# Two of four softmax attentions get a ring of four sequences instead of three, and their row maxima are scored 11 slots sooner

## The chip, the cores and the metric

The kernel runs on one core of one Trainium2 chip. The metric is the device time of one execution in microseconds. The engines are TensorE (PE, matmuls), VectorE (DVE), ScalarE (ACT), GpSimd (POOL) and SyncE (SP, which here only issues DMAs).

## The reference, cut to what matters

Four transformer layers on `x`, 16 sequences of 256 tokens by 128 features. Each layer is `x + gate * attention(norm(x))`, then `x + gate * ffn(norm(x))`; layer 2's second half is itself a small transformer layer with a second attention. The change touches the attention of layer 0 (called a0) and that inner attention of layer 2 (a4). Both are causal, with 16 heads of 8 features:

```
q, k, v = h @ wq, h @ wk, h @ wv            # a4: 4 key/value heads, rotary embedding on q and k
s    = where(causal, q @ k.T / sqrt(8), -inf)   # 256 x 256, for 16 sequences x 16 heads
attn = softmax(s)                               # a4; a0 has per-head gates folded into q
out  = (attn @ v) @ wo
```

## The kernel before

`attention_phase` runs one attention over all 16 sequences as a software pipeline. Every engine executes the same hand-written order: a function `step(t, m)` for one step `t`, which is a loop over slots `h` = 0 to 15. In slot `h` of step `t` each engine does what is planned there for sequences at different stages: `has(stage, t)` says whether sequence `t + stage` exists. Waits are `after(engine, signal, b, k)`, and each engine executes its list strictly in order. Steps -3 to 0 and 13 to 16 are written out; steps 1 to 12 are a hardware loop of four passes over three steps (`steps`). The places in SBUF form a ring of three (`m`, `t % 3`): `QH`, `KH` (queries and keys with their mask rows), `VX` (values), `H`, `CX`.

For one sequence, in order of stages:

- **Norm**, step b-3, slots 4 to 12: PE mean (L669), DVE `XC`, ACT `SQ`, PE variance (L674), DVE `VE`, POOL `RS`, DVE `DG`, PE broadcast (L680), DVE `XN` (L841), ACT `H` (L523).
- **Projection and split**, step b-2, from slot 0: PE q and k (L656/L657; with rotary embedding L653/L654 twice), DVE (L810 on; rotary L804/L805 and POOL L469), then in slot 4 ACT splits q and k into three bf16 parts in the single buffer `SPL` (L536, POOL L475, ACT L539, POOL L478). SP copies these into `QH`/`KH` with 6 DMAs (L436/L437) and, when those have landed, duplicates them inside with 6 more (L442/L444); the first issue of a sequence is L435. The signal for "all landed" is `parts_sent`. The ACT split of the next sequence waits for it, since `SPL` is single.
- **Maxima**, step b-1: PE computes scores (L587 to L589) of one head into one of three banks and DVE reduces them to row maxima `NM3` (L784, `maxima`). 16 heads lie in slots 0 to 12 (`score_slots=13`), so slots 4, 8 and 12 hold two and slots 13 to 15 none. In slots 8 (heads 0-7) and 13 (heads 8-15) DVE makes `NMQ`; two slots later PE turns them (L728), and three slots later ACT and DVE split them into `M2` (L559, L881) and POOL, after a tiny operation `GO` (L485), sends them into two rows of `QH` (L487). The signals are `m_sent[0]` and `m_sent[1]`.
- **Softmax**, step b: PE computes the transposed scores with the maxima already subtracted through those rows (`scores_t`, L605 to L607), ACT takes the exponential (L549), PE multiplies by the values (L628, `values`) every fourth slot, and output parts are turned (L635), divided (DVE L764/L770), projected (L707, L712) and added (DVE L873/L876) in the following slots and step b+1.

In slot 0 of step t, PE does, in this order:

```
after(pe, m_sent[0], t)        # scores_t(t, head 0): maxima of heads 0-7 landed in QH
after(pe, parts_sent, t + 1)   # scores(t + 1, head 0): parts of the next sequence landed
after(pe, h_ready, t + 2)      # projection of the one after
```

The `fill` copies on DVE (L740) write the constant mask rows of each ring place once.

Of the kernel before, what the change touches and what calls it, by code (L numbers as in the profile page):

```python
# [11 lines left out]
P = 128  # L12
F32 = mybir.dt.float32
BF16 = mybir.dt.bfloat16
ALU = mybir.AluOpType
# [244 lines left out]
def attention_phase(c, cfg):  # L260
# [24 lines left out]
    SCALE = float(HD) ** -0.5  # L285
    l = cfg["layer"]
    SRC, DST = cfg["src"], cfg["dst"]

    with ExitStack() as ctx:
        sb = lambda name, shape, dt=F32: c.sb(cfg["name"] + name, shape, dt, ctx)  # L290
        QH = sb("QH", [KROWS, 3, NH, T], BF16)
        KH = sb("KH", [KROWS, 3, HK, T], BF16)
        VX = sb("VX", [P, 3, 2 * SV // PK, 2 * PK, 16])
        PR = sb("PR", [P, 8, NC])
        XC, SQ, XN = (sb(n, [P, T]) for n in ("XC", "SQ", "XN"))
        H = sb("H", [P, 3, T])
# [12 lines left out]
        CX = sb("CX", [P, 3, 2, cfg["CW"] // VW, VW])  # L309
# [102 lines left out]
        @block.sync  # L412
        def _(sp):
            for dst, src in ((QC, "qrows"), (KC, "krows")):
                sp.dma_start(dst[32:P, :].bitcast(F32), c.ins[src if causal or dst is KC else "norows"]).then_inc(rows_in, 16)
            for dst, src in loads:
                sp.dma_start(dst, c.ins[src]).then_inc(w_in, 16)

            def step(t, m):
                if isinstance(t, int) and -2 <= t <= 0:  # L420
                    sp.wait_ge(zeroed, 2)
                    sp.wait_ge(rows_ready, 4 * (t + 2) + 2)
                if has(2, t):
                    b, j = t + 2, (m + 2) % 3
                    for r in range(R):
                        after(sp, st_ready, b - 3)
                        heads = slice(16 * r, 16 * r + 16)
                        kheads = slice(16 * r, 16 * r + min(HK, 16))
                        group = lambda n: slice(HD * n, HD * n + HD)
                        first_q, first_k = (0, 2, 4), (0, 1, 3)  # L430
                        for a, ready, sent in ((0, hi_ready, high_sent[r]), (1, mid_ready, mid_sent[r]), (2, lo_ready, parts_sent[r])):
                            after(sp, ready, b, r + 1)
                            if r == a == 0:
                                for z in range(2):
                                    sp.dma_start(QH[MAX0 + z:MAX0 + z + 1, j, :, :], ZR[:, :]).then_inc(parts_sent[0].sem, 16)  # L435
                            sp.dma_start(QH[group(first_q[a]), j, heads, :], SPL[:, r, a, 0, :]).then_inc(sent.sem, 16)  # L436
                            sp.dma_start(KH[group(first_k[a]), j, kheads, :], SPL[0:KR, r, a, 1, :]).then_inc(sent.sem, 16)  # L437
                        for a, sent in ((0, high_sent[r]), (1, mid_sent[r])):
                            after(sp, sent, b)
                            for n, pair in enumerate(PAIRS):  # L440
                                if pair[0] == a and n != first_q[a]:
                                    sp.dma_start(QH[group(n), j, heads, :], QH[group(first_q[a]), j, heads, :]).then_inc(parts_sent[r].sem, 16)  # L442
                                if pair[1] == a and n != first_k[a]:
                                    sp.dma_start(KH[group(n), j, kheads, :], KH[group(first_k[a]), j, kheads, :]).then_inc(parts_sent[r].sem, 16)  # L444
            steps(sp, step)

        @block.gpsimd
        def _(pool):
# [7 lines left out]
            def step(t, m):  # L456
                for h in range(NH):
                    if has(3, t):
                        b = t + 3
# [4 lines left out]
                    if has(2, t):  # L464
                        b = t + 2
# [14 lines left out]
                    for g in range(2):  # L480
                        back = L_HALF[g] // NH
                        if h == L_HALF[g] % NH and has(1 - back, t):
                            after(pool, mlo_ready, t + 1 - back, g + 1)
                            after(pool, go, t + 1 - back, g)
                            nc.gpsimd.tensor_tensor(GO[:, :], c.HALF[0:1, 0:2], c.HALF[0:1, 0:2], ALU.add).then_inc(go.sem, 1)  # L485
                            for a in range(2):
                                pool.dma_start(QH[MAX0 + a:MAX0 + a + 1, (m + 1 - back) % 3, g * HG:(g + 1) * HG, :], M2[:, g, a, :])\  # L487
                                    .then_inc(m_sent[g].sem, 16)
# [7 lines left out]
        def _(act):  # L496
# [12 lines left out]
            def step(t, m):  # L509
                for h in range(NH):  # L510
                    if has(3, t):
                        b = t + 3
# [6 lines left out]
                        if h == L_H:  # L519
                            after(act, xn_ready, b)  # L520
                            after(act, v_ready, b - 3)
                            scale, shift = (c.MOD[:, l, 1, one(b)], c.MOD[:, l, 0, one(b)]) if centered else (COL[:, 3:4], 0.0)
                            nc.scalar.activation(H[:, m, :], XN[:, :], ACT.Identity, bias=shift, scale=scale).then_inc(h_ready.sem, 1)  # L523
                    if has(2, t):
                        b = t + 2
                        if h == L_V + 1 and not cfg.get("bv"):
                            after(act, v_ready, b)
                            if isinstance(t, int) and t == -2:
                                act.wait_ge(vx_ones, 1)
                            after(act, pv_done, b - 3)  # L530
                            nc.scalar.copy(v_place((m + 2) % 3), v_source).then_inc(v_copied.sem, 1)
# [8 lines left out]
                    if has(-1, t):  # L540
                        b = t - 1
                        if diff and h == L_COMBINE:
                            after(act, dif_ready, b)
                            nc.scalar.activation(CSQ[:, :, :, :], CX[:, (m - 1) % 3, :, :, :], ACT.Square).then_inc(csq_ready.sem, 1)
# [25 lines left out]
        def _(pe):  # L570
# [6 lines left out]
            def scores(b, j, h):  # L577
# [3 lines left out]
                if h == 0 and isinstance(b, int) and b < 2:  # L581
                    pe.wait_ge(rows_ready, 4 + 8 * b)
# [55 lines left out]
            def step(t, m):  # L638
                for h in range(NH):
                    if has(0, t):  # L640
                        scores_t(t, m, h)
                    if has(1, t):
                        for n in heads_at(h):
                            scores(t + 1, (m + 1) % 3, n)
                    if has(2, t):
                        b, j = t + 2, (m + 2) % 3
# [18 lines left out]
                    if has(3, t):  # L665
                        b = t + 3
# [15 lines left out]
                    if burst_at(h) and has(burst_at(h)[1], t):  # L682
                        u, back = burst_at(h)
                        values(t + back, (m + back) % 3, u)
                    for s, back in late(h, turn_at):
                        if has(-back, t):
# [4 lines left out]
                            for g in range(2):  # L691
                                if turns_before(L_NMQ[g] + 2) == s and has(1 - back, t):
                                    after(pe, mlo_ready, t + 1 - back, g + 1)
                            turn(b, s)
                    if has(-1, t):
                        b = t - 1
                        if h == L_CTT:
# [6 lines left out]
                            for n in range(2):  # L704
                                for r in range(R2):
                                    src = CX[:, (m - 1) % 3, n, :, :].rearrange("p h d -> p (h d)")[:, r * P:(r + 1) * P]
# [7 lines left out]
                    for g in range(2 if has(1, t) else 0):  # L714
                        b = t + 1
                        if h == L_NMQ[g] + 2:
# [4 lines left out]
                            if has(0, t):  # L721
                                after(pe, cx_ready, t, turns_before(L_NMQ[g] + 2))
# [10 lines left out]
        def _(v):  # L733
# [56 lines left out]
            def step(t, m):  # L790
                for h in range(NH):
                    if has(2, t):
                        b = t + 2
                        for n in range(QK):
                            if h == L_QK[n] + 1:
                                if isinstance(t, int) and t == -2 and n == 0:
# [19 lines left out]
                        if h == L_V + 1 and cfg.get("bv"):  # L816
                            after(v, v_ready, b)
                            if isinstance(t, int) and t == -2:
                                v.wait_ge(vx_ones, 1)
                            after(v, pv_done, b - 3)  # L820
                            bv = BV[:, :].rearrange("p (h d) -> p h d", h=SV).unsqueeze(1).to_broadcast([P, 2, SV, VW])
                            v.tensor_tensor(v_place((m + 2) % 3), v_source, bv, ALU.add).then_inc(v_copied.sem, 1)
                    if has(3, t):
                        b = t + 3
# [18 lines left out]
                    if has(1, t):  # L843
                        b = t + 1
                        for n in heads_at(h):
                            maxima(b, n)
                        for g in range(2):
                            heads = slice(g * HG, (g + 1) * HG)
                            if h == L_NMQ[g] and causal:
# [4 lines left out]
                    if has(-1, t):  # L854
# [7 lines left out]
                        if diff and h == L_CTT - 1:  # L862
                            after(v, cr_ready, b)
                            cx = CX[:, (m - 1) % 3, :, :, :]
# [17 lines left out]
                    for s, back in late(h, turned_at):  # L882
                        if has(-back, t):
                            turned(t - back, (m - back) % 3, s)
# [1058 lines left out]
def build(nc, ins, out):  # L1943

    with ExitStack() as ctx:
# [8 lines left out]
        attention_phase(c, dict(ln, name="a0", score_slots=13, layer=0, NH=16, HK=16, HV=16, VW=8, CW=128, causal=True,  # L1954
# [13 lines left out]
        attention_phase(c, dict(name="a4", score_slots=13, layer=2, centered=False, eps=rms["neps"], NH=16, HK=16, HV=4, VW=8, CW=128,  # L1968
# [115 lines left out]
```

## Time and profile before

| | us |
|---|---|
| median of 3 runs (lowest, highest) | 4036.28 (4019.64, 4040.5) |
| the profiled execution, its span | 4006.55, 4004.7 |
| a0: first head score to last value matmul | 65.1 to 389.8 |
| a4: first head score to last value matmul | 2481.6 to 2863.9 |

Busy time of an engine says how much work it has; what matters for a pipelined phase is how long one step takes and what PE waits for at its start. The granted clock of TensorE is 1.00 at 2.4 GHz and 0.50 at 1.2 GHz.

### The profile page before, as it was taken

Reading aid. Unit: us, or ns where it says so; the run is one execution under the profiler, and the core shown is the slowest. Engines: PE = TensorE matmul, PEld = TensorE weight load, DVE = VectorE, ACT = ScalarE, POOL = GpSimd, SP = SyncE. Lnnn points to the kernel's source line nnn. Section 1 sums busy time; section 2 is a strip of 40 time slices with the busy share of each in tenths; the row PEclk is TensorE's granted clock in tenths of the full one; section 3 lists DMA queues with packets and bytes.
Section 4 is the critical chain, followed back from the end, with each engine's and each line's share of the span. In section 5 each row is a group of like instructions: output and inputs, shape, how many; then the busy total and the mean of one; then the engine's idle time right before and its main releaser. Section 6 shows DMA issues by size and latency. Waiting matters only on the chain. (4 is left out here: it accounts for less than half of the span.)

```text
span 4004.7 us, 71964 instructions
## 1 busy us (share of the span) xinstructions
PE 3023.2 (75%) x20738; PEld 1870.4 (47%) x20738; DVE 2388.8 (60%) x5571; ACT 1445.8 (36%) x3108; POOL 915.0 (23%) x976
## 2 busy tenths in 40 slices
PE   5787433158888876999978986777779984459799
PEld 4555433146655653444435554555634461145344
DVE  5665841178887854333347765555555579984555
ACT  2555100026555534333326661444432221113321
POOL 2222118633333320000002222223200034430000
PEclk6899766569999988999989996888889985569899
DMA  3332313434333310000001111222100000000000
GB/s 70 41 42 42 109 38 55 63 63 53 44 48 45 41 49 3 1 0 0 0 8 27 23 19 21 34 33 35 39 2 0 0 3 0 0 5 22 4 0 21
DMA packets 125781, 111.13 MB, mean 28 GB/s; under 512 B 25177, under 2 KB 115938, under 8 KB 121570
## 3 DMA queue, kind: packets, MB, share of 16 engines
q1 hardware_dynamic: 103474, 93.91, 13.7%
q0 software_dynamic: 20912, 12.58, 2.1%
q8 instruction: 127, 2.08, 0.2%
q10 hardware_dynamic: 1152, 1.61, 0.1%
q14 instruction: 116, 0.95, 0.1%
HBM read 35.28 MB, written 13.86 MB: 12 GB/s over the span
## 5 line engine op out<-in xcount | busy, mean ns | idle before, releaser
L1408 DVE TENSOR_TENSOR f1eHS<-f1eSG,bank 128x512 f32<-128x512 f32 x256 | 175.9, 687 | 319.8 <-PE bank L1336 234.5
L1314 PE MATMUL bank<-f1NT,f1W 128*128 (+1 forms) x576 | 296.4, 596 | 15.8 <-DMA f1eSELB<-in_sel 15.3
L549 ACT ACTIVATE a1PR<-bank 128x384 f32<-128x384 f32 x512 | 242.8, 493 | 149.0 <-PE bank L607 145.1
L1336 PE MATMUL bank<-f1eHS,f1W 128*128 128x512 f32 x576 | 293.8, 592 | 0.0
L784 DVE TENSOR_REDUCE a1NM<-bank 128x3 f32<-128x384 f32 x512 | 262.8, 549 | 28.4 <-PE bank L589 25.7
L1367 ACT ACTIVATE f1eSG<-bank,f1eFB 128x512 f32<-128x512 f32 x256 | 175.8, 687 | 283.5 <-PE bank L1314 161.7
L784 DVE TENSOR_REDUCE a4NM<-bank 128x3 f32<-128x384 f32 x256 | 132.9, 551 | 136.8 <-PE bank L589 134.7
L787 DVE TENSOR_REDUCE a2NMQ<-bank 128x2 f32<-128x512 f32 x256 | 168.1, 685 | 60.6 <-PE bank L593 60.4
L953 PE MATMUL bank<-ONES 128*128 128x256 bf16 x960 | 172.0, 287 | 24.2 <-DMA f3nWR<-in_wr 4.6
L784 DVE TENSOR_REDUCE a0NM<-bank 128x3 f32<-128x384 f32 x256 | 133.8, 551 | 94.7 <-PE bank L589 93.5
L549 ACT ACTIVATE a4PR<-bank 128x384 f32<-128x384 f32 x256 | 122.3, 489 | 187.0 <-PE bank L607 186.4
L549 ACT ACTIVATE a2PR<-bank 128x512 f32<-128x512 f32 x256 | 149.6, 596 | 91.6 <-PE bank L611 89.5
L1314 PEld LDWEIGHTS bank<-f1NT,f1W 128*128 128x128 f32 x576 | 109.2, 191 | 156.2 <-issue 154.5
L1336 PEld LDWEIGHTS bank<-f1eHS,f1W 128*128 128x128 f32 x576 | 109.4, 190 | 130.1 <-issue 120.3
L549 ACT ACTIVATE a0PR<-bank 128x384 f32<-128x384 f32 x256 | 121.7, 490 | 133.5 <-PE bank L607 132.8
L1502 POOL TENSOR_TENSOR lM<-lF,lV 128x1024 f32<-128x1024 f32 x32 | 122.2, 3819 | 166.7 <-DVE lF L1515 166.2
L605 PE MATMUL bank<-a1QH,a1KH 128*128 128x128 bf16 x512 | 116.6, 229 | 57.0 <-ACT a1PR L549 42.6
L1367 ACT ACTIVATE f2eSG<-bank 128x512 f32<-128x512 f32 x96 | 57.3, 597 | 192.9 <-PE bank L1314 179.7
L1403 DVE TENSOR_TENSOR f3eT<-f3eSG,bank 128x512 f32<-128x512 f32 x88 | 60.5, 688 | 107.3 <-PE bank L1317 97.0
L1367 ACT ACTIVATE f3eSG<-bank 128x512 f32<-128x512 f32 x88 | 52.6, 597 | 190.0 <-PE bank L1314 190.0
L449 POOL MEMSET a2ZR<- 16x256 bf16 x1 | 0.3, 302 | 526.5 <-POOLq L1262 526.5
L953 PEld LDWEIGHTS bank<-ONES 128*128 128x128 bf16 x960 | 100.6, 119 | 42.5 <-issue 8.5
(633 smaller groups left out, 8613.5 us busy)
## 6 DMA issues: line engine op xcount, KB each, us to landing
a1QH<-a1SPL SPq DMA_DIRECT2D x96, 64.0 KB
a1KH<-a1SPL SPq DMA_DIRECT2D x96, 64.0 KB
a1QH<-a1QH SPq DMA_DIRECT2D x96, 64.0 KB
a1KH<-a1KH SPq DMA_DIRECT2D x96, 64.0 KB
f1W<-in_w SPq DMA_DIRECT2D x2, 2304.0 KB, 10.8
sums<-rZT SPq DMA_DIRECT2D x2, 2112.0 KB
sW<-in_w SPq DMA_DIRECT2D x1, 4096.0 KB, 12.5
xLD<-sums SPq DMA_DIRECT2D x16, 256.0 KB, 5.7
```

What stands on the lines that cost most here:

```text
L449: nc.gpsimd.memset(ZR[:, :], 0.0).then_inc(zeroed, 1)
L549: nc.scalar.activation(PR[:, h % 8, :], bank[2 + h % 2][:, 0:NC], ACT.Exp, scale=SCALE)\
L605: pe.matmul(o[:, 0:P], k(0), q(0), start=True, stop=True)
L784: v.tensor_reduce(NM3[:, h, :], S_BANK[h % 3][:, 0:NC].rearrange("p (n k) -> p n k", n=3), AX, ALU.max, negate=True).then_inc(s_used.sem, 1)
L787: v.tensor_reduce(NMQ[:, :, h], S_BANK[h % 3][:, 0:NC].rearrange("p (n k) -> p n k", n=2), AX, ALU.max, negate=True).then_inc(s_used.sem, 1)
L953: pe.matmul(bank[7][:, 0:2 * P], spare[:, 0:P], spare[:, :], start=True, stop=True)
L1314: pe.matmul(bank[q][:, :], W1[:, m * P:(m + 1) * P], x, start=True, stop=True).then_inc(g_ready.sem, 1)
L1336: mm = pe.matmul(bank[6 + j][:, :], W2[:, m, :], HS[:, m % 4, :], start=(m == 0), stop=(m == NCH - 1 and CBF is None))
L1367: nc.scalar.activation(dst, bank[q][:, :], fn, bias=FB[:, m:m + 1] if cfg.get("hbias") else 0.0)\
L1403: v.tensor_tensor(T1[:, :], a, bank[2 + q][:, :], ALU.mult).then_inc(t1_ready.sem, 1)
L1408: v.tensor_tensor(HS[:, m % 4, :], a, bank[4 + (j * NBC + kth[m]) % 2][:, :], ALU.mult).then_inc(hs_ready.sem, 1)
L1502: nc.gpsimd.tensor_tensor(M1[:, j, :, :, :], fk, vv, ALU.mult).then_inc(m1.sem, 1)
```

## The change

For a0 and a4 alone (`ring=4`, `score_slots=16`), the ring has four places, norm runs in step b-4, projection and split in step b-3, and the maxima's scores start 11 slots sooner: heads 0 to 10 of sequence t+2 in slots 5 to 15 of step t, and heads 11 to 15 of sequence t+1 in slots 0 to 4, one head in every slot. The maxima of heads 0-7 go out in slot 0 of step b-1 (they did in slot 11), those of heads 8-15 in slot 11 of step b-1 (they did in slot 0 of step b); the slots with `NMQ`, turn, `M2` and POOL DMAs stay 8/10/11 and 13/15/0, only which half of the heads uses them changes. Written out are steps -4 to 0 and 9 to 16; the loop has two passes over four steps. The other two attentions keep ring 3 and their order.

```diff
+    RING = cfg.get("ring", 3)
+    FRONT = RING - 1
-        QH = sb("QH", [KROWS, 3, NH, T], BF16)
+        QH = sb("QH", [KROWS, RING, NH, T], BF16)
...
+        LOOPS = (NB - 1 - RING) // RING
         def steps(eng, step):
-            for t in range(-3, 1):
-                step(t, t % 3)
-            with eng.Fori(0, 4) as i:
-                for k in range(1, 4):
-                    step(i * 3 + k, k % 3)
-            for t in range(13, 17):
-                step(t, t % 3)
+            for t in range(-RING, 1):
+                step(t, t % RING)
+            with eng.Fori(0, LOOPS) as i:
+                for k in range(1, RING + 1):
+                    step(i * RING + k, k % RING)
+            for t in range(LOOPS * RING + 1, 17):
+                step(t, t % RING)
...
-        L_SCORES = 0
+        L_SCORES = 0 if RING == 3 else -11
+        scores_at = lambda h: [(n, a) for a in (1, 2) for n in heads_at(h - NH * (a - 1))]
+        LAST_FILLED = 1 if RING == 3 else 2
-        L_NMQ = [16, 28] if diff else [8, 13]
+        L_NMQ = [16, 28] if diff else [8, 13] if RING == 3 else [-3, 8]
+        ahead = lambda slot: 1 - slot // NH
...
# SP, ACT, DVE, PE: projection, split and DMAs move from has(2, t) to has(FRONT, t), norm from has(3, t) to has(RING, t)
# PE, and in the same way maxima() on DVE:
-                    if has(1, t):
-                        for n in heads_at(h):
-                            scores(t + 1, (m + 1) % 3, n)
+                    for n, a in scores_at(h):
+                        if has(a, t):
+                            scores(t + a, (m + a) % RING, n)
...
# PE, turn of the maxima:
-                            if g:
-                                after(pe, mlo_ready, b, g)
+                            if g or RING > 3:
+                                after(pe, mlo_ready, b - (g == 0), 1 if g else 2)
...
-                            fill(t + 4, (part,))
+                            fill(t + RING + 1, (part,))
...
-        attention_phase(c, dict(ln, name="a0", score_slots=13, layer=0, ...
+        attention_phase(c, dict(ln, name="a0", score_slots=16, ring=4, layer=0, ...
-        attention_phase(c, dict(name="a4", score_slots=13, layer=2, ...
+        attention_phase(c, dict(name="a4", score_slots=16, ring=4, layer=2, ...
```

## Rows read from the trace of the kernel before

**Rows 1.** Busy time by stretch: a2 (the third attention), a0, a4.

```profile
core 0: us, PE busy (x) PEld busy (x) DVE busy (x) ACT busy (x) POOL busy (x), PEclk, DMA share, GB/s
...
2112.00:2402.00 290.00, 261.68 (x2438) 160.92 (x2436) 217.69 (x470) 192.17 (x388) 79.53 (x134) 0.98 0.14 23
85.00:390.00 305.00, 241.35 (x2930) 178.98 (x2929) 194.06 (x516) 168.65 (x401) 80.43 (x134) 0.92 0.28 39
2503.00:2864.00 361.00, 263.82 (x2963) 191.40 (x2963) 196.30 (x531) 162.64 (x401) 99.31 (x162) 0.86 0.24 33
```

**Rows 2.** PE's waits in a0, then in a4: us in total, times, longest.

```profile
PE bank L605 <- DMA a0QH<-a0M: 31.7, 14, 4.0
PE bank L680 <- DVE a0DG L837: 12.9, 12, 1.1
PE bank L635 <- DVE a0M L881: 10.0, 15, 0.7
...
PE bank L605 <- DMA a4QH<-a4M: 53.8, 15, 4.0
...
PE bank L587 <- DMA a4KH<-a4KH: 7.0, 7, 3.2
```

**Rows 3.** SP's first DMA issue of a sequence, by time: start, duration.

```profile
88.29 1.71 SPq L435 DMA_DIRECT2D a0QH<-a0ZR  x2
...
249.63 1.18 SPq L435 DMA_DIRECT2D a0QH<-a0ZR  x2
...
347.73 1.18 SPq L435 DMA_DIRECT2D a0QH<-a0ZR  x2
...
2512.64 1.18 SPq L435 DMA_DIRECT2D a4QH<-a4ZR  x2
...
2654.85 1.18 SPq L435 DMA_DIRECT2D a4QH<-a4ZR  x2
...
2821.86 1.19 SPq L435 DMA_DIRECT2D a4QH<-a4ZR  x2
```

**Rows 4.** Timeline at slot 0 of steps of a0 and a4: start, duration, idle before.

```profile
265.48 0.23 PE L605 MATMUL bank<-a0QH,a0KH 128*128 128x128 bf16 x1 [0.73 <-DMA a0QH<-a0M]
...
2664.22 1.09 POOL L487 DMA_DIRECT2D a4QH<-a4M  x2 [0.25 <-issue]
...
2669.81 0.29 PE L605 MATMUL bank<-a4QH,a4KH 128*128 128x128 bf16 x1 [3.52 <-DMA a4QH<-a4M]
...
2834.48 0.22 PE L605 MATMUL bank<-a4QH,a4KH 128*128 128x128 bf16 x1 [3.03 <-DMA a4QH<-a4M]
...
2837.49 0.26 PE L587 MATMUL bank<-a4KH,a4QH 128*128 128x128 bf16 x1 [2.68 <-DMA a4KH<-a4KH]
```

**Rows 5.** Landing of a4's maxima DMAs issued in 2663 to 2667, then 2671 to 2675.

```profile
DMA to landing us min/median/max: 2.2/3.6/5.0
...
DMA to landing us min/median/max: 1.6/1.6/1.6
```

**Rows 6.** Stretches (columns of rows 1): a0, its wait; a4 cold, warm, waiting.

```profile
226.10:243.20 17.10, 14.61 (x190) 11.07 (x190) 13.18 (x35) 10.87 (x26) 5.55 (x9) 1.00 0.37 48
243.20:245.00 1.80, 0.00 (x0) 0.00 (x0) 0.00 (x0) 0.00 (x0) 0.00 (x0) 0.87 0.01 2
2646.00:2651.00 5.00, 4.88 (x33) 3.04 (x34) 2.10 (x5) 1.22 (x3) 1.93 (x4) 0.51 0.01 2
2651.00:2666.30 15.30, 12.59 (x162) 9.58 (x160) 11.15 (x31) 9.28 (x23) 4.98 (x7) 1.00 0.35 43
2666.30:2669.80 3.50, 0.00 (x0) 0.00 (x0) 0.00 (x0) 0.03 (x1) 0.00 (x0) 0.74 0.17 42
```

**Rows 7.** SP's first issue of a sequence in a2, steps 1 to 6 of its loop.

```profile
2134.79 1.18 SPq L435 DMA_DIRECT2D a2QH<-a2ZR  x2
2153.27 1.18 SPq L435 DMA_DIRECT2D a2QH<-a2ZR  x2
2172.09 1.18 SPq L435 DMA_DIRECT2D a2QH<-a2ZR  x2
2190.60 1.19 SPq L435 DMA_DIRECT2D a2QH<-a2ZR  x2
2209.08 1.19 SPq L435 DMA_DIRECT2D a2QH<-a2ZR  x2
2227.58 1.19 SPq L435 DMA_DIRECT2D a2QH<-a2ZR  x2
```

**Rows 8.** The ramp of a0: first scores, second split, first softmax matmul.

```profile
65.06 0.29 PE L587 MATMUL bank<-a0KH,a0QH 128*128 128x128 bf16 x1 [7.86 <-DMA a0KH<-a0KH]
...
68.20 0.62 ACT L536 CAST a0SPL<-a0QKF 128x512 bf16<-128x512 f32 x1 [9.91 <-DVE a0QKF L815]
...
84.12 0.29 PE L605 MATMUL bank<-a0QH,a0KH 128*128 128x128 bf16 x1 [3.99 <-DMA a0KH<-a0KH]
```

**Rows 9.** DVE in a0: a maximum, a norm operation, a fill of the keys' rows.

```profile
L784 DVE TENSOR_REDUCE a0NM<-bank 128x3 f32<-128x384 f32 x164 | 86.2, 552 | 53.3 <-PE bank L589 52.5
...
L841 DVE TENSOR_TENSOR a0XN<-a0XC,bank 128x256 f32<-128x256 f32 x10 | 4.2, 421 | 0.0
...
L740 DVE COPY a0KH<-a0KC x6: 1216/1222/1354, 31.4 to 57.7; 32x4096 bf16<-32x4096 bf16 x3, 64x4096 bf16<-64x4096 bf16 x3
```

**Rows 10.** Steps 14 and 15 of a0, without projection, norm and copies.

```profile
363.50:378.80 15.30, 13.99 (x178) 9.85 (x178) 10.87 (x28) 8.92 (x22) 2.37 (x6) 0.89 0.01 3
378.80:391.50 12.70, 9.62 (x135) 5.68 (x132) 2.82 (x9) 8.23 (x21) 1.19 (x3) 0.99 0.02 3
```

More of the change, by code:

```diff
@@ L308, in attention_phase @@
         RC = sb("RC", [P, 2, 4 * PK])
[L309 removed]
+        CX = sb("CX", [P, RING, 2, cfg["CW"] // VW, VW])
         CTT = sb("CTT", [P, R2, T])
@@ L419, in step @@
             def step(t, m):
-                if isinstance(t, int) and -2 <= t <= 0:
+                if isinstance(t, int) and -FRONT <= t <= 0:
                     sp.wait_ge(zeroed, 2)
-                    sp.wait_ge(rows_ready, 4 * (t + 2) + 2)
-                if has(2, t):
-                    b, j = t + 2, (m + 2) % 3
+                    sp.wait_ge(rows_ready, 4 * (t + FRONT) + 2)
+                if has(FRONT, t):
+                    b, j = t + FRONT, (m + FRONT) % RING
                     for r in range(R):
-                        after(sp, st_ready, b - 3)
+                        after(sp, st_ready, b - RING)
                         heads = slice(16 * r, 16 * r + 16)
@@ L457, in step @@
                 for h in range(NH):
-                    if has(3, t):
-                        b = t + 3
+                    if has(RING, t):
+                        b = t + RING
                         if h == L_VE:
@@ L463, in step @@
                             nc.gpsimd.tensor_tensor(RS[:, :], VE[:, :], c.HALF[:, 0:2], ALU.pow).then_inc(rs_ready.sem, 1)
-                    if has(2, t):
-                        b = t + 2
+                    if has(FRONT, t):
+                        b = t + FRONT
                         for n in range(2 if rope else 0):
@@ L510, in step @@
                 for h in range(NH):
-                    if has(3, t):
-                        b = t + 3
+                    if has(RING, t):
+                        b = t + RING
                         if h == L_SQ:
@@ L580, in scores @@
                     after(pe, parts_sent[h // 16], b)
-                if h == 0 and isinstance(b, int) and b < 2:
-                    pe.wait_ge(rows_ready, 4 + 8 * b)
+                if h == 0 and isinstance(b, int) and b <= LAST_FILLED:
+                    pe.wait_ge(rows_ready, 4 * RING if b == LAST_FILLED else 4 * (b + 1))
                 o = S_BANK[h % 3]
@@ L664, in step @@
                             mm.then_inc(v_ready.sem, 1)
-                    if has(3, t):
-                        b = t + 3
+                    if has(RING, t):
+                        b = t + RING
                         if h == L_MEAN and centered:
@@ L683, in step @@
                         u, back = burst_at(h)
-                        values(t + back, (m + back) % 3, u)
+                        values(t + back, (m + back) % RING, u)
                     for s, back in late(h, turn_at):
@@ L691, in step @@
                             for g in range(2):
-                                if turns_before(L_NMQ[g] + 2) == s and has(1 - back, t):
-                                    after(pe, mlo_ready, t + 1 - back, g + 1)
+                                a = ahead(L_NMQ[g] + 2)
+                                if turns_before((L_NMQ[g] + 2) % NH) == s and has(a - back, t):
+                                    after(pe, mlo_ready, t + a - back, g + 1)
                             turn(b, s)
@@ L713, in step @@
                             mm.then_inc(o_ready.sem, 1)
-                    for g in range(2 if has(1, t) else 0):
-                        b = t + 1
-                        if h == L_NMQ[g] + 2:
+                    for g in range(2):
+                        a = ahead(L_NMQ[g] + 2)
+                        if h == (L_NMQ[g] + 2) % NH and has(a, t):
+                            b = t + a
                             if causal:
@@ L791, in step @@
                 for h in range(NH):
-                    if has(2, t):
-                        b = t + 2
+                    if has(FRONT, t):
+                        b = t + FRONT
                         for n in range(QK):
                             if h == L_QK[n] + 1:
-                                if isinstance(t, int) and t == -2 and n == 0:
+                                if isinstance(t, int) and t == -FRONT and n == 0:
                                     v.wait_ge(zeroed, 2)
@@ L817, in step @@
                             after(v, v_ready, b)
-                            if isinstance(t, int) and t == -2:
+                            if isinstance(t, int) and t == -FRONT:
                                 v.wait_ge(vx_ones, 1)
-                            after(v, pv_done, b - 3)
+                            after(v, pv_done, b - RING)
                             bv = BV[:, :].rearrange("p (h d) -> p h d", h=SV).unsqueeze(1).to_broadcast([P, 2, SV, VW])
-                            v.tensor_tensor(v_place((m + 2) % 3), v_source, bv, ALU.add).then_inc(v_copied.sem, 1)
-                    if has(3, t):
-                        b = t + 3
+                            v.tensor_tensor(v_place((m + FRONT) % RING), v_source, bv, ALU.add).then_inc(v_copied.sem, 1)
+                    if has(RING, t):
+                        b = t + RING
                         if h == L_MEAN + 1 and centered:
@@ L842, in step @@
                                             ALU.mult).then_inc(xn_ready.sem, 1)
[L843 to L847, printed above, removed]
+                    for n, a in scores_at(h):
+                        if has(a, t):
+                            maxima(t + a, n)
+                    for g in range(2):
+                        if has(ahead(L_NMQ[g]), t):
+                            b = t + ahead(L_NMQ[g])
                             heads = slice(g * HG, (g + 1) * HG)
-                            if h == L_NMQ[g] and causal:
+                            if h == L_NMQ[g] % NH and causal:
                                 after(v, s_used, b, HG * (g + 1))
```

38 lines of the change are left out of this document (19 added, 19 removed).

## The prediction

> **What bounds the kernel now.** I read the busy time by stretch first. PE is busiest in a0 and a4, but only 79% and 73% of the time, at a granted clock of 0.92 and 0.86; a2, the same program with nearly no copies of keys, is at 90% and 0.98 [rows 1]. PE is the bound, then, and something stops it. The list of PE's waits names it: in a0 31.7 us, in a4 53.8 us go to the DMAs that put the maxima into QH, about once per step and always at slot 0, and a4 has 7.0 us more on the copied parts [rows 2].
>
> The length of a step comes from SP's first issue of a sequence. In a0 13 steps take 347.73 - 88.29 = 259.4 us, 19.96 each; in a4 2821.86 - 2512.64 = 309.2 us, 23.79 each [rows 3].
>
> Why these lengths? ACT's split (0.62 us, just before SP's first issue) sets off 12 copies, and slot 0 of the next step begins when they are over: in a0 split at 249.0, PE goes on at 265.48, 16.5 us later; in a4 split at 2654.2, PE at 2669.81, 15.6 us later [rows 3, 4]. The maxima of heads 0-7, issued in slot 11 amid the copies, land late with them (2.2 to 5.0 us, against 1.6 alone) [rows 5]. One boundary shows both waits apart: maxima at 2834.48, parts at 2837.49, 16.2 us after their split [rows 3, 4]. So before, a step is a closed chain: slot 0, projection, split (3 to 4 us later in a0, some 8 in a4), 16 us of copies, slot 0. Moving the maxima alone would do little; the parts stand right behind them.
>
> The wait costs twice. After it a4 runs 5.0 us at clock 0.51 before it has 1.00 again; nearly all of that PE is busy [rows 6].
>
> **The change, part by part.**
>
> *Maxima of heads 0-7* go out at slot 0, 16 slots before their use instead of 5; those of heads 8-15 in slot 11, 13 before theirs instead of 8. The slowest landing seen, 5.0 us, is hidden by at least 13 slots of about 1 us each. The wait of [rows 2] on M goes, at both places.
>
> *Parts* were needed 12 slots after the split (slot 4 to slot 0) and are now needed 17 slots after it (slot 4 to slot 5 of the next step), about one whole step. They need 15.6 to 16.5 us. With a step of 17 or more they are there with 1 to 2 us to spare. Their other reader is the next split, since SPL is single: split to split can't be under about 16.5 us. That is the floor of a step, in both.
>
> *The step without its wait.* a0: from 226.1 to 243.2, 17.10 us, the clock is 1.00 and all that a step does is done; the rest of that step is 1.80 us of nothing [rows 6]. So 17.1. PE is busy 14.6 of it, DVE 13.2, ACT 10.9; the other gaps are DG (12.9 us in 12) and M2 (10.0 in 15) [rows 2, 6], in slots that the change leaves in place. a4: 15.3 us at full clock, plus 5.0 at half that PE fills, which is 2.5, gives 17.8; DVE's and POOL's rotary operations in there don't shrink with the clock, so I take 18.0 (18.8 if only half of the 2.5 comes back, 17.6 as the low end).
>
> *One head per slot* adds no work: 16 reductions of 0.55 us [rows 9] a step as before. Slots 4, 8 and 12 lose one, slots 13 to 15 get one. Slot 8 is that of VE and TMP, ahead of DG, so PE's wait of 1.1 us there may shrink by up to 0.55; in slots 13 to 0 the reductions stand before NMQ and M2, and could delay the turns that wait for them (0.7 us each now) by as much. Bounds -0.5 and +1.6 us per step (three handovers); I take 0, since DVE has 4 us of slack in the step.
>
> *The ramp.* In step -2 DVE has, from 65.1 on, 11 maxima (6.1), four fills of the added ring place (4.9) and some six norm and NMQ operations of at most 0.42 (2.0): to 78. The first slots of step -1 hold 5 maxima, two projection copies and M2 (4.0): to 82. The second sequence's parts are no obstacle: their split waited for its projection until 68.2, which now stands ahead of the scores, so it starts at 65.1 and they land at 81 [rows 8]. Then 11 maxima, norm, NMQ and M2 (9.2): to 91 [rows 9]. Softmax starts at 91 instead of 84.1: 7 us later, in each of the two; the larger memsets and the first fills lie under the loads and the first copies. Low end 4 (the fills hidden in waits), high end 10.
>
> *The end.* Full steps are 0 to 11 now, one less than before. Step 12 has no norm (15.5 by the norm's PE time and DG's wait off 17.1). Step 13 is like the old step 14: 15.3 at clock 0.89, 13.6 at full [rows 10]. Step 14 has 5 maxima's scores instead of 16; since the step without any still takes 12.7 [rows 10], 13.0. Step 15 stays 12.7.
>
> *Code.* Six more steps' instructions are written out and two loop passes go. In a2 the backward branch lies between the third and fourth issue: 18.51, beside 18.48, 18.82, 18.48 and 18.50 [rows 7]. So nothing for either.
>
> The Trainium skill (Runtime: NRT & Kernel Launch, "Instruction fetch mechanics") says that a taken branch out of the buffered pages costs a fetch stall and straight code doesn't; by it two stalls fewer per attention would come on top, and these rows show no such stall to win.
>
> **The sum.** a0: 91 + 12 x 17.1 + 15.5 + 13.6 + 13.0 + 12.7 = 351.0 against 391.5 [rows 10]: -40.5. a4: softmax starts at 2509 instead of 2502, + 12 x 18.0 + 16.5 + 13.6 + 13.0 + 12.7 = 2780.8 against 2865.3 (its last matmul's end): -84.5. Together -125 us. Nothing else of the kernel changes. The profiled execution took 4006.55 us (span 4004.7), so it would take 3882; the median of the runs is 4036.28, 30 above it, and I put the same 125 us there: **3911 us**.
>
> **Rivals.**
>
> *A. The copies keep the pace, less tightly (0.12).* If the chain split, copies, next split takes 18.5 us instead of 16.5, because the copies now follow each other with hardly a pause (DMA share 0.28 in a0 now, 0.33 then) and share the queues with the maxima, a0 has 18.5 and a4 18.5 per step: 12 x 1.4 + 12 x 0.5 = 23 us back, 3934; with 20 us, 12 x 2.9 + 12 x 2.0 = 59 back, 3970. For it: 16.5 is only 0.6 below a0's step. Against: in the step of [rows 6] the copies ran beside all of PE's work already.
>
> The Trainium skill (DMA: Bandwidth & Descriptors, "Issuing engines are not separate DMA queues") says that DMAs of all engines interleave on the same 16; the late landing of the maxima among the copies agrees (3.6 against 1.6 us). By it the maxima still land late and slow the copies as they do now.
>
> *B. DVE's order in slots 13 to 0 (0.12).* All three handovers late by one reduction: 1.65 us x 12 x 2 = 40 back, 3951.
>
> *C. No change (0.04).* If PE's wait at slot 5 took the place of that at slot 0, for instance because the split moved later by as many slots as the use, the steps would stay 19.96 and 23.79, and the ramps cost 14: 4050, +0.35%. Against: the split's slot is the same, its reader is 5 slots later.
>
> *D. Slower (0.03).* The same single buffer, from a worse price: each microsecond of the split-to-split cycle over 19.96 in a0 and 23.79 in a4 costs 13 each; with the ramps' 14 it decides at about 0.3 us over both (+20 us is 0.5%). If landing took 22 us in a0 and 24.5 in a4: 14 + 26 + 9 = 49 slower, 4085. Against: nothing now shows more than 16.5.
>
> *E. More than forecast (0.04).* a0 at its floor of 16.5 and a4 at 17.2 with a ramp of 4: another 7 + 10 + 6 us, 3888.
>
> **How the numbers follow.** The forecast has 0.65. Its own range: steps of 16.5 to 17.6 and 17.6 to 18.8, ramps of 4 to 10, so -143 to -103 us, on a base of 4006 to 4040: 3863 to 3937. A and B reach to 3970; without their far end 3866 to 3962 leaves 2 in 10 out. Measured differences under 0.5% (20 us) can't be told from none here. The cases give faster 0.93 (forecast, A, B, E), same 0.04, slower 0.03.
>
> **What would show it.** Right: PE's waits on M gone from both phases, those on KH under 5 us; SP's first issues about 17.1 and 18.0 us apart; clock above 0.97 in both; first L605 of a0 about 91. Wrong: ACT's split waiting for the copies (A), L635 or L728 waiting longer on DVE (B), L587 on KH at slot 5 (C, D).

## The result, and the profile after

The changed kernel takes 3903.62 us (median of 4 runs, 3900.47 to 3928.53); the kernel before takes 4027.96 us beside it (median of 4 runs, 4007.57 to 4040.5). The ratio, estimated from all these runs, is 0.971, with a 95% interval of 0.9649 to 0.977. By the medians it is 124 us faster, where 125 were forecast. The profiled execution took 3906.53 us (span 3904.5), 100.0 us less than that of before.

The line numbers of after are 7 to 10 higher: L605 is L612, L587 is L594, L635 is L642, L680 is L687, L435 is L442, L536 is L543, L549 is L556.

Where the 100 us came from can be read from the first fill of the zero row (ZR) to the last matmul of the values in each phase. a0 lies at the start of the kernel: its last value matmul began at 389.8 and begins at 357.1, so 32.7 us less. a4 took 419.4 us (2444.5 to 2863.9) and takes 341.9 (2429.3 to 2771.2): 77.5 less. a2 isn't touched, and took 16.2 us more (336.6, now 352.8), because its clock was low in more of its steps in this execution (seven steps of 19.8 to 22.9 us, where the profile of before has one of 20.0). All the rest together is 6 us shorter. So it is 110 us from the two changed phases, where the sum of the prediction had 125.

Busy time by stretch of the kernel after: a0, a4, and two times 20 us of a2. This answers to [rows 1].

```profile
core 0: us, PE busy (x) PEld busy (x) DVE busy (x) ACT busy (x) POOL busy (x), PEclk, DMA share, GB/s
95.00:357.00 262.00, 218.66 (x2854) 163.25 (x2857) 186.19 (x492) 160.97 (x393) 75.27 (x127) 0.97 0.32 44
2496.00:2772.00 276.00, 228.77 (x2909) 170.32 (x2906) 188.50 (x509) 159.86 (x396) 93.49 (x154) 0.98 0.31 42
...
2060.00:2080.00 20.00, 14.57 (x58) 8.51 (x59) 12.41 (x25) 3.80 (x7) 4.22 (x6) 0.50 0.17 27
2080.00:2100.00 20.00, 20.00 (x108) 12.05 (x106) 11.93 (x23) 8.99 (x19) 4.17 (x6) 0.53 0.14 23
```

PE's share rose from 79% to 83% in both changed phases (a4 had 73%), and the clock from 0.92 and 0.86 to 0.97 and 0.98. PE's busy time fell too, from 241 to 219 us and from 264 to 229. The stretches hold 76 and 54 matmuls fewer than those of [rows 1], which is a small part of it (some 6 and 4 us, an estimate from the mean time of one); the rest is that less of the work is done on the cold clock that followed each wait. The rows of a2 are the end of its ramp: the clock was at 0.50 already while PE was busy only 14.57 us of 20.00, and it stayed there through the next 18 us, in which PE had no pause.

PE's waits of the kernel after in a0, then in a4 (us in total, times, longest). This answers to [rows 2].

```profile
PE bank L642 <- DVE a0M L891: 13.8, 15, 1.2
PE bank L612 <- ACT a0PR L556: 12.2, 14, 5.1
PE bank L687 <- DVE a0DG L846: 8.9, 11, 1.2
PE bank L612 <- issue: 3.5, 1, 3.5
PE bank L594 <- DMA a0KH<-a0KH: 1.7, 1, 1.7
...
PE bank L642 <- DVE a4M L891: 14.3, 15, 1.2
...
PE bank L687 <- DVE a4DG L846: 7.3, 11, 1.0
PE bank L594 <- DMA a4KH<-a4KH: 5.4, 3, 3.6
PE bank L612 <- issue: 5.0, 1, 5.0
```

The waits on M's DMAs (31.7 and 53.8 us) are gone. Two lines are new. In a0 PE waits 12.2 us for ACT's exponentials (1.0 before). And in each phase there is one wait of 3.5 and 5.0 us that ends with "issue", so PE waited for nothing that the profile shows.

The first of the two is explained by ACT's own waits in a0:

```profile
ACT a0SPL L543 <- DMA a0KH<-a0KH: 17.0, 11, 5.2
```

ACT stands at its split until the copies of the sequence before have left SPL, 11 times, 1.5 us each, and the exponentials that PE needs are queued behind it.

SP's first issue of a sequence (start, duration). This answers to [rows 3].

```profile
100.98 1.18 SPq L442 DMA_DIRECT2D a0QH<-a0ZR  x2
117.56 1.19 SPq L442 DMA_DIRECT2D a0QH<-a0ZR  x2
...
168.38 1.18 SPq L442 DMA_DIRECT2D a0QH<-a0ZR  x2
189.73 1.18 SPq L442 DMA_DIRECT2D a0QH<-a0ZR  x2
...
307.86 1.18 SPq L442 DMA_DIRECT2D a0QH<-a0ZR  x2
...
2503.49 1.18 SPq L442 DMA_DIRECT2D a4QH<-a4ZR  x2
...
2573.63 1.18 SPq L442 DMA_DIRECT2D a4QH<-a4ZR  x2
2598.10 1.18 SPq L442 DMA_DIRECT2D a4QH<-a4ZR  x2
...
2720.53 1.89 SPq L442 DMA_DIRECT2D a4QH<-a4ZR  x2
```

In a0 12 steps take 307.86 - 100.98 = 206.9 us, 17.24 each (19.96 before); in a4 2720.53 - 2503.49 = 217.0, 18.09 each (23.79 before). But one step of each is much longer than the others: 21.35 us in a0 and 24.47 in a4, the fifth of the eight in the loop. The other eleven have a mean of 16.87 and 17.51.

The timeline of the kernel after, at the ramp of a0 and at the two "issue" waits (start, duration, idle before). This answers to [rows 8].

```profile
83.80 0.62 ACT L543 CAST a0SPL<-a0QKF 128x512 bf16<-128x512 f32 x1 [2.56 <-DVE a0QKF L824]
...
92.92 0.22 PE L612 MATMUL bank<-a0QH,a0KH 128*128 128x128 bf16 x1
...
100.28 0.62 ACT L543 CAST a0SPL<-a0QKF 128x512 bf16<-128x512 f32 x1 [5.24 <-DMA a0KH<-a0KH]
...
101.35 0.29 PE L612 MATMUL bank<-a0QH,a0KH 128*128 128x128 bf16 x1 [5.09 <-ACT a0PR L556]
...
185.43 0.29 PE L612 MATMUL bank<-a0QH,a0KH 128*128 128x128 bf16 x1 [3.53 <-issue]
...
2590.10 0.29 PE L612 MATMUL bank<-a4QH,a4KH 128*128 128x128 bf16 x1 [5.04 <-issue]
```

Softmax starts at 92.92. From the third split (83.80) to the fourth (100.28) it is 16.5 us, the floor that the prediction named; ACT waits 5.24 us there and PE, behind it, 5.09. The two "issue" waits stand in the two long steps, where the loop's first pass (steps 1 to 4) ends and its second (5 to 8) begins: at the backward branch. After the one at 185.43 PE runs 5 us at clock 0.50; after the one at 2590.10 the clock is 0.65 over 5 us.

### The profile page after: what moved, and what is told of

Read it like the earlier page. It is cut to its first block and busy times, and to the rows that moved or that the text cites. A ratio compares the mean times of both kernels' runs of the same rounds, so it can differ in the third digit from the quotient of the medians.

```text
span 3904.5 us, 70914 instructions
## 1 busy us (share of the span) xinstructions
PE 2996.1 (77%) x20689; PEld 1850.3 (47%) x20738; DVE 2402.7 (62%) x5579; ACT 1439.4 (37%) x3108; POOL 918.8 (24%) x976
## 5 line engine op out<-in xcount | busy, mean ns | idle before, releaser
L556 ACT ACTIVATE a1PR<-bank 128x384 f32<-128x384 f32 x512 | 242.4, 492 | 152.9 <-PE bank L614 148.8
L556 ACT ACTIVATE a2PR<-bank 128x512 f32<-128x512 f32 x256 | 149.7, 596 | 109.4 <-PE bank L618 107.4
L963 PE MATMUL bank<-ONES 128*128 128x256 bf16 x960 | 168.4, 282 | 23.3 <-DMA f3nWR<-in_wr 3.9
L612 PE MATMUL bank<-a1QH,a1KH 128*128 128x128 bf16 x512 | 116.9, 230 | 57.1 <-ACT a1PR L556 42.6
L556 ACT ACTIVATE a4PR<-bank 128x384 f32<-128x384 f32 x256 | 121.0, 489 | 98.4 <-PE bank L614 97.8
L556 ACT ACTIVATE a0PR<-bank 128x384 f32<-128x384 f32 x256 | 120.0, 489 | 82.8 <-PE bank L614 82.2
L1413 DVE TENSOR_TENSOR f2eT<-f2eSG,bank 128x512 f32<-128x512 f32 x96 | 65.9, 687 | 88.0 <-PE bank L1327 79.3
## 6 DMA issues: line engine op xcount, KB each, us to landing
f1W<-in_w SPq DMA_DIRECT2D x2, 2304.0 KB, 10.9
```

The source lines that it names most:

```text
L556: nc.scalar.activation(PR[:, h % 8, :], bank[2 + h % 2][:, 0:NC], ACT.Exp, scale=SCALE)\
L612: pe.matmul(o[:, 0:P], k(0), q(0), start=True, stop=True)
L963: pe.matmul(bank[7][:, 0:2 * P], spare[:, 0:P], spare[:, :], start=True, stop=True)
L1413: v.tensor_tensor(T1[:, :], a, bank[2 + q][:, :], ALU.mult).then_inc(t1_ready.sem, 1)
```

## The experiments

The forecast came out, but two of its steps looked doubtful: that the branch costs nothing, and that the parts alone would have kept the old pace. The kernels e1, e2, e4 and e5 shared one chip and its runs of the kernel before (median 4007.36 us beside e1), and e3, e6, e7 and e8 another (4012.56 us). Between the two groups ratios are compared, each with its 95% interval.

**e1, written out.** The changed kernel, with all steps of a0 and a4 written out, no loop:

```diff
+            if RING == 4:
+                for t in range(1, 17):
+                    step(t, t % RING)
+                return
             with eng.Fori(0, LOOPS) as i:
```

> The changed kernel, with all steps of a0 and a4 written out, no hardware loop. Theory 1 (the passes of the four-step loop cost an instruction stall of PE at the backward branch): the two idle stretches of PE put to 'issue', 3.5 us in a0 and 5.0 us in a4, go, with the cold clock behind them; the step between the fifth and the sixth loop step falls from 21.4 to about 17 us in a0 and from 24.5 to about 17.7 in a4, and the whole is 9 to 13 us shorter than the changed kernel, about 3893. Rival (the stall has another cause, such as a late DMA or a page of code that is fetched late wherever it lies): the two stretches stay or move, and the time is within 4 us of the changed kernel.

Measured: 3878.26 us (3865.32 to 3888.71, 4 runs), ratio 0.9659 (0.9599 to 0.9718), some 20 us below the changed kernel's 0.971; the intervals overlap, and the profile decides. No "issue" wait is left in a0 or a4. Softmax, from its first to its last exponential, takes 258.1 us in a4 (274.0 with the loop), and a0 ends at 347.7 (357.1): 25 us. That is more than the two long steps had too much (4.5 and 7.0 us over the mean of the others). The rest is in the ordinary steps; SP's first issues in a4:

```profile
2490.91 1.19 SPq L446 DMA_DIRECT2D a4QH<-a4ZR  x2
2507.71 1.18 SPq L446 DMA_DIRECT2D a4QH<-a4ZR  x2
2524.51 1.18 SPq L446 DMA_DIRECT2D a4QH<-a4ZR  x2
```

They are 16.80 us apart, where the ordinary steps of the changed kernel had a mean of 17.51, and those inside the loop 17.51 to 17.90. So a loop costs here in two ways: at its branch, and in each step. The expectation had only the first of them (9 to 13 us).

**e2, the ring alone.** The changed kernel with four ring places, but the maxima's scores where they were before:

```diff
-        L_SCORES = 0 if RING == 3 else -11
+        L_SCORES = 0
-        L_NMQ = [16, 28] if diff else [8, 13] if RING == 3 else [-3, 8]
+        L_NMQ = [16, 28] if diff else [8, 13]
-        attention_phase(c, dict(ln, name="a0", score_slots=16, ring=4, ...
+        attention_phase(c, dict(ln, name="a0", score_slots=13, ring=4, ...
```

(a4 likewise, and the wait on mlo_ready goes back to its old form.)

> Ring of four and one more pipeline step, but the maxima's scores where they were (slots 0 to 12 of the step before the softmax, 13 slots, maxima sent in slots 11 and 16). Theory 1 (the maxima's own DMAs, issued in slot 11 amid the copies and landing with them, hold PE at slot 0 just as the parts do): PE still waits for M at slot 0 in nearly every step, a0's step stays at 18.5 to 20 us and a4's at 21 to 23.8, so that the whole is 3960 to 4040 us, at most half of the gain. Rival (the parts were the real limit and the maxima only stood in front of them): the wait falls under 1 us a step and the time is near that of the changed kernel, 3900 to 3930.

Measured: 4012.94 us (4002.39 to 4032.88, 10 runs), ratio 0.9999 (0.9971 to 1.0026): nothing. PE's waits in a0 and a4:

```profile
PE bank L612 <- DMA a0QH<-a0M: 28.1, 12, 4.5
...
PE bank L612 <- DMA a4QH<-a4M: 42.6, 12, 4.3
```

[rows 2] had 31.7 and 53.8. With the parts out of the way, the maxima alone keep the steps in the loop of a0 at 19.3 to 20.8 us (22.75 at the branch) and in that of a4 at 23.1 to 24.4; their DMAs, issued in slot 11 amid the copies, take 3.5 us to land (two issued at 2609.05, median), and PE goes on at 2614.52. Both waits end at slot 0, and taking away one of them is worth nothing.

**e3, the kernel before written out.** The same edit as e1's, on the kernel before.

> The kernel before (ring of three), with all steps of a0 and a4 written out. Theory 1 (before, whatever the loop costs was hidden in PE's wait for the copies and maxima at slot 0, so writing out is worth something only once that wait is gone): within 12 us of the kernel before, steps of 19 to 20 us in a0 and 23 to 23.8 in a4. Rival (writing out is worth its 20 us by itself, in either kernel): 15 to 30 us shorter than the kernel before.

Measured: 4011.46 us (4001.51 to 4044.8, 10 runs), ratio 1.0015 (0.9979 to 1.0051). The steps stay at 18.7 to 20.5 and 23.1 to 24.4 us. So what the loop costs in each step lay under the wait for the DMAs before, and came out only when that wait went. The gain of e1 needs the change.

**e4, thirteen slots.** The changed kernel with score_slots=13 in place of 16, the one edit "one head per slot" undone.

> The changed kernel with the maxima's scores still 11 slots sooner but in 13 slots again, so three slots hold two heads and three none. Theory 1 (one head per slot is worth nothing by itself): within 10 us of the changed kernel, 3895 to 3915. Rival (the even order is what lets PE run through, since double heads make PE wait on DVE in slots 9 and 10): 15 to 40 us slower than the changed kernel, with L687 and L594 waiting longer on DVE.

Measured: 3914.02 us (3909.59 to 3922.73, 4 runs), ratio 0.9735 (0.9676 to 0.9794), 10 us above the changed kernel and within both intervals. a0 ends 2.9 us later than after; a4's steps in the loop are 18.2 to 19.6 us instead of 17.5 to 17.9, and PE waits longer there for what DVE makes:

```profile
PE bank L669 <- DVE a4RES L814: 7.4, 13, 0.6
```

(2.9 us in 13 with one head per slot). So a maximum less in slots 4, 8 and 12 helps the rotary work of a4, which in all takes 8.5 us more here (from the zero row's first fill to the last value matmul). The size, about 10 us, isn't settled by the times. PE's wait on DG is not what improved: it is 6.2 us in 11 in a0 with thirteen slots, and 8.9 in 11 with sixteen.

**e5, two splits.** The changed kernel with two buffers SPL, used in turn, and a semaphore for each; ACT's split waits for the copies of the sequence two back, not one:

```diff
-        SPL = sb("SPL", [P, R, 3, 2, T], BF16)
+        SPL = sb("SPL", [P, 2 if RING == 4 else 1, R, 3, 2, T], BF16)
-                                after(act, parts_sent[r], b - 1)
+                                after_parts(act, r, b - (2 if RING == 4 else 1), sp2(m))
```

> The changed kernel with two buffers for the split parts (SPL) and two semaphores for the landed parts, so that ACT's split waits for the copies of the sequence two before. Theory 1 (a0's step stands at the floor set by the single buffer, 16.3 to 17.4 us, of which ACT's split waits 17.0 us in 11 steps): the wait of ACT's split on KH goes, a0's step falls by 0.3 to 0.8 us and the stall of 5.2 us at the first softmax step goes; 5 to 14 us shorter than the changed kernel, 3890 to 3898. Rival (PE's own work sets 16.9 us and ACT's wait lies beside it, or the copies themselves can't go faster and PE then waits for the parts at slot 5): within 4 us of the changed kernel.

Measured: 3901.41 us (3889.25 to 3908.61, 4 runs), ratio 0.9699 (0.9636 to 0.9761), the same as the changed kernel within the intervals. In the profile a0 ends at 347.8, 9.3 us earlier: ACT's wait for the copies is gone, and PE's wait for the exponentials falls from 12.2 to 1.4 us. a4 is 3 us longer than after, and the 5 to 14 us that were expected of the whole don't show in the times. The stall of 5 us in the ramp stays, as one of 4.2 us at slot 5 of step 0. The profile names no releaser for it, but PE goes on at 100.43, 17.9 us after the third split (82.51), about when its parts land; so I read it as the wait for the parts, which nothing but an earlier third split would shorten. That of 3.5 us at the branch stays too.

**e6, written out with two splits.** e1 and e5 together.

> The changed kernel with a0 and a4 written out and two buffers for the split parts. Theory 1 (the single buffer is what holds a0's written-out step at 16.2 to 17.0 us, with 16.2 us of ACT's split waiting for the copies): a0's steps fall to 15.6 to 16.2 us, a4's stay at 16.8, and the whole is 4 to 12 us shorter than with the writing out alone (3878), about 3870. Rival (the copies themselves, 12 issues of SP and their traffic, can't repeat faster than every 16.2 us, so PE waits for the parts at slot 5 instead): within 3 us of 3878.

Measured: 3859.28 us (3851.62 to 3864.68, 4 runs), ratio 0.9617 (0.9565 to 0.967). SP's first issues in a0:

```profile
156.30 1.18 SPq L454 DMA_DIRECT2D a0QH<-a0ZR  x2
171.91 1.28 SPq L454 DMA_DIRECT2D a0QH<-a0ZR  x2
187.54 1.18 SPq L454 DMA_DIRECT2D a0QH<-a0ZR  x2
203.15 1.18 SPq L454 DMA_DIRECT2D a0QH<-a0ZR  x2
```

A step of a0 takes 15.6 us, under the 16.5 of the single buffer (e1, which has it, shows 16.2 to 17.0), and a0 ends at 330.1, 17.6 us earlier than in e1: more than the 4 to 12 us expected. a4 stays at 16.80: there the buffer was no bound.

**e7, a loop of six steps.** The kernel before, with a2's loop as two passes of six steps instead of four of three, and nothing else:

```diff
-            with eng.Fori(0, 4) as i:
-                for k in range(1, 4):
-                    step(i * 3 + k, k % 3)
+            BODY = 6 if cfg["name"] == "a2" else 3
+            with eng.Fori(0, 12 // BODY) as i:
+                for k in range(1, BODY + 1):
+                    step(i * BODY + k, k % 3)
```

> The kernel before, with the loop of a2 (the attention that waits for no copies) as two passes over six steps instead of four over three. Theory 1 (a backward branch stalls PE by some 4 us when the loop's body is longer than what the engine holds of its instructions, and not with three steps): one idle stretch of PE of 3 to 6 us put to 'issue' at the seventh step of a2's loop, one step of 22 to 25 us among steps of 18.5, a2 4 to 7 us longer. Rival (the stall belongs to the ring of four or its waits, not to the length of the body): all of a2's loop steps stay at 18.5 us, but for clock dips.

Measured: 4015.93 us (4011.09 to 4051.22, 10 runs), ratio 1.0018 (0.9989 to 1.0047): too little to time. But a2, which had no such step behind any of its three branches (18.51, 18.51 and 18.55 us), has one now, the seventh, just behind its single branch:

```profile
2229.39 1.18 SPq L436 DMA_DIRECT2D a2QH<-a2ZR  x2
2252.21 1.18 SPq L436 DMA_DIRECT2D a2QH<-a2ZR  x2
```

The wait that it holds, from the list of a2's waits:

```profile
PE bank L611 <- issue: 3.5, 1, 3.5
```

Same ring, same steps, same branch, only more code between the branch and where it goes: 22.82 us instead of 18.5, with the clock at 0.50 for the 5 us behind the wait. So it is the length of the loop's body, not the ring of four. e2 agrees from the other side: its bodies of four steps have such waits too, 4.1 us in a0 and 4.2 in a4, with the maxima where they were.

**e8, everything written out.** e6 with a1 and a2 written out too; the condition `if RING == 4` becomes `if True`.

> As the kernel with a0 and a4 written out and two split buffers, and the steps of a1 and a2 (ring of three) written out as well. Theory 1 (inside a loop each step costs 0 to 1 us more, since waits are against registers: 17.8 against 16.8 in a4, where PE is the bound; but 18.5 against 18.25 in a2): a2 0 to 4 us shorter, a1 0 to 8 us, the whole 0 to 12 us under the same kernel with a1 and a2 in loops. Rival (more straight code costs fetches, or nothing): no difference, or some us longer.

Measured: 3815.85 us (3806.17 to 3836.5, 4 runs), ratio 0.9522 (0.9462 to 0.9582), the fastest here: 88 us below the changed kernel by the medians, though not beside it, and 43 us below e6 on the same chip, where at most 12 were expected. Its busy time in a0 and a4:

```profile
core 0: us, PE busy (x) PEld busy (x) DVE busy (x) ACT busy (x) POOL busy (x), PEclk, DMA share, GB/s
99.00:331.00 232.00, 207.17 (x2838) 158.42 (x2837) 180.57 (x486) 158.18 (x386) 72.25 (x124) 1.00 0.35 48
2421.00:2672.00 251.00, 216.76 (x2866) 164.00 (x2867) 183.14 (x499) 157.40 (x391) 90.25 (x149) 1.00 0.33 45
```

PE is at 89% and 86%, at full clock. a1's softmax takes 533.8 us instead of 567.2 in the kernel before (566.9 in e6), which is most of the gain over e6, and a2's steps 18.11 instead of 18.50. The trace of before already had the warning, in a1's list of waits (a1's loop has three steps of 32 slots, and three backward branches):

```profile
PE bank L605 <- issue: 10.9, 3, 3.9
```

## Why the prediction came out, and where it was off

**What bounds it: right, with one wrong sentence.** The closed chain at slot 0 was the bound, and both halves of the change were needed. But "Moving the maxima alone would do little; the parts stand right behind them" says only half of it. e2 shows the other half: moving the parts alone does nothing, since the maxima, which are issued amid the copies, land with them. The maxima alone can't be tried without the ring place, because their scores need the parts a step sooner; that half stays argued.

**The waits on M and KH: right.** M's are gone, and the parts now cost 1.7 us in a0 and 5.4 in a4 (under 5 forecast).

**The step without its wait: 17.1 and 18.0 forecast, 17.24 and 18.09 measured, but by two errors that cancel, which is luck.** The ordinary steps are shorter (16.87 and 17.51), and one in each phase is longer (by 4.5 and 7.0 us). For a4 the low end of 17.6 was the better estimate of an ordinary step; written out it is 16.8.

**Code: wrong.** "So nothing for either" was read from a2, whose loop body has three steps of 16 slots; the changed phases got a body of four. The branch costs PE 3.5 and 5.0 us and the cold clock behind it; by the lengths of the two steps it is 4.5 and 7.0 us, some 11 in all. The body grew from three steps to four, and the prediction, which counted the written-out steps, put no price on that. e1 takes the stall away, e3 shows that in the kernel before there was nothing of it to win, and e7 makes it in a2 by the length of the body alone. The Trainium skill (Runtime: NRT & Kernel Launch, "Instruction fetch mechanics") says that a taken branch to code outside the buffered pages stalls until that code is fetched, and calls the cost of straight code mostly hidden. The runs agree: short body no stall, long body a stall of 3.5 us, the same steps written out none. The prediction had it, and set it aside on rows that were right for their loop only; a1's 10.9 us would have decided it the other way.

**The floor by the single SPL: there, and a0 stands on it, but it isn't a fixed 16.5 us.** ACT's 17.0 us of waiting show where it acts, and e6 gets below it with a second buffer. In a0 ACT's split went on as soon as the copies had landed 16.3 to 17.9 us behind the split before, 16.9 in the mean, and in e1 16.2 was enough in several steps; the prediction had read 15.6 to 16.5. So this is the mechanism of rival A at a small part of its price (18.5): with hardly a pause between them the copies often take somewhat longer than was read before, and their mean is the length of a0's ordinary step, 16.87. What the prediction didn't name is who pays: ACT is blocked at the split, and PE waits for the exponentials behind it (12.2 us).

**One head per slot: about as forecast or a little better.** PE's wait on M2 rose (10.0 to 13.8 us in 15), 0.25 us per step, so rival B did not come. That on DG fell (12.9 to 8.9), but not for the reason given: with two heads in slots 4, 8 and 12 it fell further (6.2, e4). e4 puts the edit at 10 us of gain, which its interval doesn't settle; the low bound of -0.5 us per step would be 12 over the 24 steps.

**The ramp: 7 us forecast, 8.6 and 8.7 measured** by the first exponential (84.7 to 93.3 in a0, and 58.1 to 66.8 behind the zero row's first fill in a4). In a0 the prediction missed the single buffer here: the second split, at 66.18, waits 6.58 us for the first sequence's copies, not for its projection, and the third is as late as 83.80. The fourth, due at slot 4 of the first step, waits 5.24 us, so the first issue of that step comes 8.1 us after softmax starts (100.98 - 92.92) instead of 4.2 (88.29 - 84.12).

**The sum.** a0 gave 32.7 of 40.5 us; missing are 1.6 of the ramp, 3.9 of the first step, 1.7 of twelve steps. a4 gave 77.5 of 84.5; missing are 1.7 of the ramp and 5.3 in the stretch, where 24.47 us stand for one step of 18.0. The medians moved by 124 us; part of their agreement with 125 is luck, as the profiled execution has 110 from the two phases. The median of before stands on four runs from 4007.57 to 4040.5; the 13 and 19 runs of the same kernel beside the experiments have medians of 4007.36 and 4012.56.

**Rivals C, D and E** did not come: PE hardly waits at slot 5 for the parts (1.7 us in a0, 5.4 in a4, in four waits together), the slowest landing seen took some 17.9 us, where D needed 22 and 24.5, and the ramps were longer, not shorter.

## What to carry to other kernels

Before a wait is removed, list everything that ends at the same point: here maxima and parts both ended at slot 0, and removing one was worth nothing (ratio 0.9999) where both gave 0.971. A wait of several microseconds per step also hides what lies under it, such as slower steps in a loop, waits at its branch, or a single buffer, and each comes out at once when it goes; after such a change look for "issue" waits and for engines queued behind a buffer's release. When a cost is read from a neighbouring loop, read it from the one whose body is as long as the new one will be.

## What the runs showed of the hardware

A backward branch cost PE nothing visible behind a body of 3 steps of 16 slots (a2, [rows 7]), 3.5 and 5.0 us behind 4 such steps (3.5 to 5.6 over a0 and a4 of the changed kernel, e2, e4 and e5), 3.5 us behind 6 (e7), and 10.9 us in three, 3.9 at most, behind 3 steps of 32 slots (a1). In the 5 us behind such a wait the clock was 0.50 in a0, in a1 (0.50 to 0.53) and in e7, and 0.65 in a4.

Steps in a loop were longer than the same steps written out, apart from the branch: 17.51 to 17.90 against 16.80 us in a4, 18.50 against 18.11 in a2. In one and the same kernel, e5's a0 has 16.20 and 16.20 us in the last two full steps of its loop and 15.62, 15.60 and 15.62 in the last three written out behind it. The written-out steps wait on constants and the loop's on values in registers, which may be the cause; no run here separates it, and it stays open.

The granted clock of a2, which the change doesn't touch, was low in most of the kernels run here, for up to seven steps of 19.5 to 23.3 us instead of 18.5. Some of it can be read from the changed kernel's trace. Once low, the clock can stay at 0.50 for some 18 us of work without a pause (2080 to 2098), where behind the branch of a0 it was back after 5. The falls inside a2 come right after slots in which PE had gaps (columns of [rows 1]):

```profile
2116.00:2118.00 2.00, 1.42 (x12) 1.30 (x13) 2.00 (x7) 0.76 (x3) 0.00 (x0) 1.00 0.29 35
2118.00:2120.00 2.00, 1.40 (x10) 0.87 (x7) 2.00 (x5) 1.59 (x4) 0.51 (x2) 0.77 0.02 6
2120.00:2130.00 10.00, 10.00 (x60) 4.17 (x59) 3.36 (x9) 4.00 (x8) 3.12 (x6) 0.53 0.02 4
```

The gaps are PE's waits on DG and M (0.73 and 0.60 us, ending at 2116.58 and 2119.20). But the same two waits (0.72 and 0.60, ending at 2239.62 and 2242.24) are followed by no fall. What decides between the two is open. In e8's a1 such a dip comes with every fourth step: 35.95 us at a mean clock of 0.91, beside 33.53 us at 1.00.
